# Two prototype mixtures rewritten as a pipeline over blocks, and the experts' first loads moved under the normalisation

## What is computed

```python
x = x + 0.5 * experts(ln(x))
x = x + delta_attention(ln(x))
x = x + 0.5 * experts(ln(x))
x = x + 0.5 * mixture(ln(x))
x = x + helical_attention(ln(x))
x = x + 0.5 * mixture(ln(x))

def experts(x):                    # 8 experts, gates from the mean over a sequence's tokens
    logits = x.mean(axis=1) @ gate_w.T + gate_b
    gates = softmax(where(logits < second largest, -inf, logits))
    return einsum('be,beso->bso', gates, gelu(einsum('bsd,eod->beso', x, expert_w) + expert_b))

def mixture(xf):                   # 32 prototypes, rank 16, the two nearest for each token
    d2 = sum(xf * xf) + sum(p * p) - 2 * xf @ p.T
    w = softmax(-sqrt(max(d2, 0)) / max(abs(temp), 0.1))
    topw, topi = top_k(w, 2);  topw = topw / sum(topw)
    for s in range(2):
        out += topw[s] * (A[topi[s]] @ (B[topi[s]] @ xf) + bias[topi[s]])
    return out
```

## Time and profile before

| | us |
|---|---|
| median of 3 runs | 4886.96 (4878.78 to 4890.54) |
| the profiled execution | 4886.68 |
| its span | 4884.9 |

### The profile page before, as it was taken

One profiled execution on the slowest core, in us unless ns is written; L12 is line 12 of the kernel. 1 busy time (PEld: TensorE's weight loads), 2 busy tenths in 40 slices (PEclk: granted clock), 3 DMA queues, 4 the chain that ended last, 5 costly groups with the idle time before them and its releaser, 6 DMA issues. The chain is left out here.

```text
span 4884.9 us, 64394 instructions
## 1 busy us (share of the span) xinstructions
PE 3811.3 (78%) x16142; PEld 1479.4 (30%) x16142; DVE 3865.6 (79%) x5725; ACT 3062.1 (63%) x4245; POOL 1846.0 (38%) x1828
## 2 busy tenths in 40 slices
PE   7986002656556896987589999999999999999468
PEld 3432001545443342342122222222222222222123
DVE  5536697999994663368789999999999999998352
ACT  5568101222222563337469999999999999999242
POOL 1000683666661101106424444444444444444112
PEclk9999555777778998989889999999999999999789
DMA  1013545444442000024511111111011111110300
GB/s 45 9 48 87 72 88 117 102 89 100 97 93 73 11 7 11 0 81 155 169 30 31 34 38 38 38 37 38 23 37 37 38 38 38 37 22 5 112 10 35
DMA packets 126458, 265.24 MB, mean 54 GB/s; under 512 B 41296, under 2 KB 70864, under 8 KB 117904
## 3 DMA queue, kind: packets, MB, share of 16 engines
q1 hardware_dynamic: 124208, 252.56, 21.6%
q10 hardware_dynamic: 1952, 9.18, 0.6%
HBM read 170.26 MB, written 91.26 MB: 54 GB/s over the span
## 5 line engine op out<-in xcount | busy, mean ns | idle before, releaser
L1032 POOL TENSOR_TENSOR att_heads_rest<-att_heads_probs,att_heads_high 128x352 f16<-128x352 f32 x1024 | 873.5, 853 | 1242.3 <-DVE att_heads_rest L1184 1182.6
L1164 DVE TENSOR_REDUCE att_heads_maxima<-att_heads_peek 128x1 f32<-128x1024 f32 x992 | 1209.1, 1219 | 42.3 <-PE att_heads_peek L1059 42.3
L1132 ACT ACTIVATE att_heads_probs<-att_heads_scores 128x1024 f32<-128x1024 f32 x1024 | 1057.8, 1033 | 171.2 <-PE att_heads_scores L1078 153.7
L1078 PE MATMUL att_heads_scores<-att_heads_q,att_heads_k 128*128 128x512 f16 (+1 forms) x4096 | 1075.2, 385 | 32.1 <-issue 28.8
L1134 ACT ACTIVATE att_heads_high<-att_heads_scores 128x1024 f16<-128x1024 f32 x1024 | 1054.5, 1030 | 0.0
L1184 DVE TENSOR_TENSOR att_heads_rest<-att_heads_probs,att_heads_high 128x672 f16<-128x672 f32 x1024 | 882.9, 862 | 69.1 <-POOL att_heads_rest L1032 55.4
L1903 PE MATMUL delta_scan_sums<-delta_scan_o_terms,main_identity 128*128 128x256 f32 x1536 | 412.7, 437 | 604.4 <-POOL delta_scan_o_terms L1971 604.4
L1059 PE MATMUL att_heads_peek<-att_heads_k,att_heads_q 112*128 112x512 f16 x1984 | 599.9, 383 | 18.2 <-DVE att_heads_maxima L1164 17.1
L1903 PEld LDWEIGHTS delta_scan_sums<-delta_scan_o_terms,main_identity 128*128 128x128 f32 x1536 | 340.9, 224 | 676.5 <-POOL delta_scan_o_terms L1971 617.6
L1078 PEld LDWEIGHTS att_heads_scores<-att_heads_q,att_heads_k 128*128 128x128 f16 (+1 forms) x4096 | 319.2, 98 | 708.1 <-issue 461.2
L1094 PE MATMUL att_heads_out<-att_heads_high,att_heads_v_head 128*64 128x512 f16 x2048 | 418.6, 405 | 15.3 <-DVE att_heads_rest L1184 14.7
(11 more groups left out here) (247 smaller groups left out, 4677.0 us busy)
## 6 DMA issues: line engine op xcount, KB each, us to landing
delta_scan_record<-delta_record SPq DMA_DIRECT2D x64, 898.0 KB, 9.4
att_heads_q<-att_hel SPq DMA_DIRECT2D x192, 128.0 KB, 3.1
att_heads_k<-att_hel SPq DMA_DIRECT2D x192, 128.0 KB, 3.2
att_hel<-att_hel_high SPq DMA_DIRECT2D x32, 512.0 KB, 4.4
att_hel<-att_hel_rest SPq DMA_DIRECT2D x32, 512.0 KB, 5.0
delta_record<-delta_chunks_record SPq DMA_DIRECT2D x64, 224.5 KB, 4.3
att_o<-att_heads_out_copy SPq DMA_DIRECT2D x256, 32.0 KB
att_out_parts<-att_o ACTq DMA_DIRECT2D x8, 1024.0 KB, 15.7
```

The source lines that it names most:

```text
L1032: nc.gpsimd.tensor_tensor(rest[:, step % 4, SPLIT:], probs[:, step % 4, SPLIT:], high[:, step % 4, SPLIT:], ALU.subtract).then_inc(rest_b_ ...
L1078: mm = nc.tensor.matmul(scores[:, step % 2, tokens(j)], k[0:rows, slot, number, tile * P:(tile + 1) * P], q[0:rows, slot, number, tokens(h ...
L1132: nc.scalar.activation(probs[:, step % 4], scores[:, step % 2], ACT.Exp, scale=LOGIT_SCALE).then_inc(probs_ready, 1)
L1164: nc.vector.tensor_reduce(maxima[:, m:m + 1], peek[:].rearrange("p j n -> p (j n)"), AX.X, ALU.max).then_inc(peek_read, 1)
```

## The change

1. In `layer_norm` POOL's part is gone; DVE forms the rest for both tiles in one instruction of 128x1024. A function `preload` can be given, which SP runs there.
2. In `gated_experts` SP issues the first two experts and the two gate tables by that function, in the normalising stage. The loop of loads begins at the second pair. PE gives its credit before its logits, and ACT rounds the first expert's weights before the gates' exponentials.
3. `prototype_mixture` no longer calls `layer_norm`. It is one stage without hardware loops. All work of a block, its mean, variance, distances, choice and shares too, is written as functions of the block (n) or the step (g), and these are called in a fixed order: the first blocks up to the first sums, and then, in the steps of block n, the mean, variance and distances of blocks n+2 and n+3 and the choice of block n+1. The choice is made for 4 tiles of 128 tokens at a time in place of 32. Distances, their transposes and the turned shares of a block use one bank, `route`; mean and variance use another, `moments`.

The core of the diff (in the mixture only lines that came in; all functions named in the order exist for ACT and DVE as well):

```diff
-def layer_norm(nc, c, stage, xn, sums, parts=None, x_loaded=None):
+def layer_norm(nc, c, stage, xn, sums, parts=None, x_loaded=None, preload=None):
...
+            @block.sync
+            def _(sp):
+                if preload is not None:
+                    preload(sp)
...
-                        nc.vector.tensor_tensor(parts[:, 1, 0, tokens(m)], xn[:, 0, tokens(m)], parts[:, 0, 0, tokens(m)], ALU.subtract)
-
-            @block.gpsimd
-            def _(pool):
-                if parts is not None:
-
-                    for n in range(NBLK):
-                        pool.wait_ge(high_ready, n + 1)
-                        nc.gpsimd.tensor_tensor(parts[:, 1, 1:, tokens(n)], xn[:, 1:, tokens(n)], parts[:, 0, 1:, tokens(n)], ALU.subtract)
+                        nc.vector.tensor_tensor(parts[:, 1, :, tokens(m)], xn[:, :, tokens(m)], parts[:, 0, :, tokens(m)], ALU.subtract)
...
+        def load_first(sp):
+
+            for slot in range(2):
+                sp.dma_start(expert[:, slot], dram["expert"][:, slot]).then_inc(expert_loaded[slot], 16)
+            for tile, table in ((gate_w, "gate_w"), (gate_b, "gate_b")):
+                sp.dma_start(tile[:], dram[table]).then_inc(tables_loaded, 16)
+
+        layer_norm(nc, c, f"{stage}_ln", xn, sums, xn_parts, x_loaded, load_first)
...
-                with sp.Fori(0, E // 2) as pair:
+                with sp.Fori(1, E // 2) as pair:
...
+                pe.sem_inc(pre_ready, CREDIT)
                 pe.wait_ge(terms_ready, 1)
...
-                pe.sem_inc(pre_ready, CREDIT)
...
+                def sums(g):
+                    if g >= STEPS:
+                        return
+                    n, m = divmod(g, RT)
+                    if m == 0:
+                        pe.wait_ge(parts_ready, n + 1)
+                        pe.wait_ge(mix_ready, n + 1)
+                    if g >= 2:
+                        pe.wait_ge(wide_ready, g - 1)
+                        pe.wait_ge(low_ready, g - 1)
...
+                mean(0)
+                variance(0)
+                mean(1)
+                distances(0)
+                variance(1)
+                turn_distances(0)
+                mean(2)
+                turn_mix(0)
+                variance(2)
+                pe.wait_ge(tables_rest, len(TABLES))
+                pe.wait_ge(tables_high, len(TABLES) + 1)
+                for g in range(AHEAD):
+                    sums(g)
+                distances(1)
+                for n in range(NBLK):
+                    for m in range(RT):
+                        g = n * RT + m
+                        if m == 0:
+                            mean(n + 3)
+                        if n == 0 and m == 1:
+                            turn_distances(1)
+                        if n == 0 and m == 2:
+                            turn_mix(1)
+                        if m == 2:
+                            variance(n + 3)
+                        sums(g + AHEAD)
+                        if n >= 1 and m == 1:
+                            turn_mix(n + 1)
+                        if m == 2:
+                            distances(n + 2)
+                        if m == 3:
+                            turn_distances(n + 2)
+                        raise_ranks(g)
...
+                nc.scalar.preload_act_table_set(LOG_EXP_SET)
+                square(0)
+                deviation(0)
+                square_normed(0)
+                square(1)
+                high(0)
                 act.wait_ge(loaded, 16 * 8)
                 for table, parts in TABLES:
                     nc.scalar.activation(parts[:, 0], table[:], ACT.Copy).then_inc(tables_high, 1)
+                root(0)
+                deviation(1)
...
+                centre(1)
+                clamp(0)
+                rest(0)
+                choose(0)
+                normalise(1)
+                weigh(0)
+                centre(2)
+                rest(1)
+                mix_rest(0)
+                normalise(2)
+                rest(2)
                 for n in range(NBLK):
+                    for m in range(RT):
+                        narrow(n * RT + m)
+                        if m == 0:
+                            if n >= 1:
+                                add(n - 1)
+                            centre(n + 3)
+                            if n == 0:
+                                clamp(1)
+                            else:
+                                choose(n + 1)
+                                weigh(n + 1)
+                        if m == 1:
+                            if n == 0:
+                                choose(1)
+                                weigh(1)
+                            else:
+                                mix_rest(n + 1)
+                        if m == 2 and n == 0:
+                            mix_rest(1)
+                        if m == 3:
+                            clamp(n + 2)
+                            normalise(n + 3)
+                            rest(n + 3)
+                add(NBLK - 1)
```

406 lines of the change are left out of this document (252 added, 154 removed).

## The result

The changed kernel takes 4812.1 us (median of 4 runs, 4808.65 to 4817.29) against 4888.75 before (4 runs, 4878.78 to 4892.28): ratio 0.9838, 95% interval 0.9825 to 0.9851. Forecast was 4820, inside a range of 4782 to 4860. The profiled execution is 4811.17 us with a span of 4809.4. The total came out as said; where it came from did not.

| stretch, us | before | after | difference | forecast |
|---|---|---|---|---|
| first experts' stage | 221.6 | 210.7 | -10.9 | -10.4 |
| delta stages, code unchanged | 1348.6 | 1344.4 | -4.2 | 0 |
| second experts' stage | 220.8 | 209.8 | -11.0 | -11.2 |
| first mixture | 244.4 | 224.9 | -19.5 | -25.4 |
| attention, code unchanged | 2597.5 | 2579.5 | -18.0 | 0 |

What follows compares the result with a forecast made beforehand. A mixture was taken to cost the sum of its stretches, with PE's own work as floor; PE also bounds the experts once it has weights. 4886.7 - 21.6 (experts) - 44.6 (mixtures) = 4820.5, stated as 4820, range 4782 to 4860.

Steps and rivals of the forecast that it cites:

- (a): Experts' normalising: without POOL in the split, DVE ends sooner, -2.9 us in each of two stages.
- (b): Experts' start: with tables and weights loaded early, PE's first product follows the split by 3.0 us, saving 7.5 and 8.3.
- PE's work: Mixture: PE's own work per block of 512 tokens is 22.4 us, 179 us for eight blocks.
- The stall: Mixture: PE waits 2.6 us once a block for DVE's `narrow`, behind centring, `choose` and `weigh`; steady blocks take 24.9.
- the walk: The prediction's step-by-step trace of the five queues through a mixture, summing to 215.3 us before the clock's cost.
- The clock: Mixture: PE's clock falls to 1.2 GHz after two stalls a mixture, costing +3.4 us, bounds 0 and +16.
- Rival B: Mixtures: the clock falls in every stall and the start is cold, 12.6 us more per mixture, 4850 us; chance 0.24.
- First sums at 32: Mixture's start: first sums come 32 us after the stage's start, bounds 24 and 42.
- Table loads: Mixture on ACT: four loads a block, 27 a mixture, 1.28 us each without a drain; only the last costs 0.4.
- Sum for the mixtures: Both mixtures fall to 218.7 us, -25.4 and -19.2, together -44.6.
- The unchanged stages: Attention and delta stages are not touched by the change, so their time changes by 0.
- Rival A: Mixtures: PE never waits, a block costs its 22.4 us, 42 us less in all, 4778 us; chance 0.15.

Runs made afterwards that it cites:

- e1: The kernel before with only the experts' half of the change, its mixture and that mixture's old layer norm kept; 4862.9 us, ratio 0.9951 to before.
- e10: e5 with ACT's square of the third block ahead moved behind the second step's evicted share sums; 4776.8 us, ratio 0.9767 to before.
- e2: The changed kernel with the old layer norm and experts, so only the mixture's half of the change; 4839.5 us, ratio 0.9904 to before.
- e3: The changed kernel with POOL again subtracting half of each block's remainder in the experts' layer norm; 4828.6 us, ratio 0.9880 to before.
- e9: The changed kernel with 243 increments of an unused semaphore on PE ahead of the attention's heads; 4835.2 us, ratio 0.9899 to before.
- e11: The changed kernel run once more, unedited; 4818.3 us, ratio 0.9856 to before.
- e4: The changed kernel with ACT copying the distances instead of taking their square root, so the walk's table loads go; 4805.2 us, ratio 0.9834 to before.
- e7: e5 with the joint Ln and Exp table loaded right behind each square root, two loads a block instead of four; 4797.3 us, ratio 0.9808 to before.
- e8: The kernel before with 486 increments of an unused semaphore on PE ahead of the attention's heads; 4938.1 us, ratio 1.0099 to before.
- e5: The changed kernel with the choice and shares of the next block issued one step later; 4792.8 us, ratio 0.9803 to before.

## Why the prediction was right, and where it was not

- **Experts, (a) and (b), -21.6**: right in mechanism and size. -10.9 and -11.0 in the trace, -24.3 in e1, which has another 2.5 us in the delta stages. The 0.68 us of a product alone, which the earlier trace rows doesn't show, is in the changed kernel's trace. The split was worth 3.7 and about 2.5 in place of 2.9, and PE's first product came 2.9 us behind it, forecast 3.0.
- **PE's work of 22.4 us a block**: e10 measures 22.26, by removing all that hides it.
- **The stall**: right in place, cause and releaser. 2.85 us against 2.6: the choice takes DVE 2.4 us against 2.25, the shares 1.35 against 1.25, since the operations on 128 columns take 0.25 to 0.35 us each. Blocks 1 to 4 took 104.1 us (1839.98 to 1944.06) against 99.6: 3.4 us of the difference are the clock and 1.3 the longer stalls. Blocks 5 to 7 took 53.0 against 49.4: 1.7 the clock, 0.5 the stalls (2.44 and 2.45 where the walk had 2.2 each), and 1.4 two waits that the walk didn't have, 0.78 for `mix_low` and 0.61 for the low parts' rest.
- **The clock, +3.4 a mixture**: mis-sized. 5.2 and 6.8 us in the changed kernel, and 6.8 to 14.8 in e2, e3, e9 and e11, whose walk is the same. "Two stalls a mixture" were in truth three and four stretches at 1.2 GHz in the changed kernel and up to six elsewhere. Rival B was half true: of the changed kernel's twelve stalls of over 2 us seven were followed by the low level.
- **First sums at 32**: measured 32.0, with the second block's deviation and its loads standing ahead as in the walk. To a tenth this is luck: the same code took 29.7 to 33.5 us in e2, e3, e9 and e11, with 3.2 to 9.4 us of it lost to the clock.
- **Table loads**: four a block at 1.283 us with no idle beside them; right, but 30 a mixture and not 27. Their price on the path, 0.4 a block, is 0.36 in e4, and 0 in another order (e7).
- **Sum for the mixtures, -44.6**: measured -31.3. This step failed in size. By the cuts of the earlier trace rows the mixtures took 224.1 and 226.1 us against 218.7, 12.8 too much: 5.2 of them are the clock (5.2 and 6.8 against 3.4 each), and the rest is in the walk, block 0 (33.8 and 34.1 us against 33), the longer stalls and the two waits of the last blocks.
- **The unchanged stages, 0**: this step failed outright. The prediction treated code as free of its place. -18 us of the -75 come from the attention, and e8 shows 15.4 of them to be bought by moving the loop's code. Without the 18 the time would have been some 4830, still in the range but on the other side of the forecast: two errors of opposite sign met, +13 in the mixtures and -22 in the unchanged stages. That the measured 4812 lies so near 4820 is luck. The delta stages' -4.2 stay open; over all kernels their time is 1344 to 1347 us with the new experts and 1348 to 1349 with POOL in the normalising, and what carries that over the stage's border was not tried.
- **Rival A** (PE never waits) was said to be barred by the centring that waits for the mean. That argument was wrong: the centring needs to stand there, but neither the choice nor ACT's square has to stand in front of the next step's product. e10 has A's steady block, 22.26 us where A had 22.4. Its 4776.8 meets A's 4778 only because the unchanged stages gave their part too: its mixtures are still longer than A's, by the start (33.5 us in the first), block 0, the waits of blocks 5 and 6 and the clock behind those.

## What to carry to other kernels

When independent work is threaded through a pipeline of in-order queues, look for the one instruction that the bound engine waits for and put everything optional behind it, on every engine of the chain that feeds it: here an ACT square held up an eviction that held up the DVE product. A stall of about 3 us on PE can cost half as much again (1.7 us behind 2.85) by the clock that falls behind it, so several equal stalls are worth more than their sum. And compare the lengths of the stages that were not edited before crediting a change with the total.

## What the runs showed of the hardware

- The jump back of a long hardware loop cost PE a stop of 2.6 to 3.3 us (4.1 to 4.5 at the first jump in the changed kernel, e3 and e5), and in one position of its code a second one of 1.3 to 2.5 us about 3 us later. Each ends 2.2 to 3.1 us behind the start of a transfer of 16384 bytes of instructions (3.8 to 4.3 at those three first jumps). With 486 instructions more ahead of the loop the six second stops were gone, and 15.4 of 2146.5 us with them (e8).
- An increment of a semaphore on PE takes 0.15 us when hundreds stand in a row (PE's pause was 54.9 us with 243 of them and 92.3 with 486).
- The same stall of 2.85 to 3.14 us was followed by full clock, by some 3.4 us at 1.2 GHz, or by 9 us of it. One program differed by 3 us a mixture from run to run in this.
- A DVE subtraction of 4 columns that takes 0.16 us alone took 1.12 when a POOL instruction of 1.16 us had begun 0.05 us before it (e5).
